# Two 16-head attentions in a four-layer kernel: order of the maxima, value projections for two pairs at a time, and the bank in which the maxima are turned

## The reference

```python
# first attention, causal
q = einsum('ahe,bce->bach', W_Q, x); k = ...W_K; v = ...W_V
scores = einsum('bach,baCh->bacC', k, q)
masked = where(causal, scores, -1e10)
attn = softmax(masked / sqrt(64)); z = einsum('bacC,baCh->bach', attn, v)
out = einsum('aeh,bach->bce', W_O, z)
x = layernorm(x + out)
# second attention of 16 heads, after the gated one
scores = einsum('bqhd,bkhd->bhqk', q, k) * (1/sqrt(16)) + rel_bias[buckets]
out = einsum('bhqk,bkhd->bqhd', softmax(scores), v).reshape(b, s, 1024) @ Wo
x = layernorm(x + out)
```

## Time and profile before

| | |
|---|---|
| median of 3 runs | 4945.93 us |
| the profiled execution | 4944.16 us, its span 4942.6 us |
| TensorE, matmuls | 4153.5 us busy (84%) |
| VectorE | 3627.2 us (73%) |
| GpSimd | 3000.0 us (61%) |
| ScalarE | 1976.0 us (40%) |
| mean granted TensorE clock | 0.926 |

### The profile page before, as it was taken

How to read it: one execution, slowest core, us unless ns; L and a number is a source line. 1 busy time by engine, 2 the same in 40 slices (tenths; PEclk the granted TensorE clock), 3 DMA queues, 4 the chain that set the end, 5 groups by cost and what they waited for, 6 DMA issues and landing times. The chain is left out here.

```text
span 4942.6 us, 63340 instructions
## 1 busy us (share of the span) xinstructions
PE 4153.5 (84%) x22330; PEld 2157.3 (44%) x22330; DVE 3627.2 (73%) x5957; ACT 1976.0 (40%) x3403; POOL 3000.0 (61%) x2548
## 2 busy tenths in 40 slices
PE   5999999999688788778778756999999999999947
PEld 3544544445354444444344323444444444444416
DVE  3877878777477677777777745888788788878735
ACT  2443434434264445345334322444344344434410
POOL 1655656556376787787778762666566566656710
PEclk6999999999889899899999976999999999999976
DMA  2000100000110000000000002212121121211120
GB/s 48 13 13 13 32 10 26 9 5 1 35 49 17 17 25 25 25 17 25 29 17 17 5 21 45 39 26 35 33 32 30 30 40 26 39 31 26 17 60 18
DMA packets 98044, 125.91 MB, mean 25 GB/s; under 512 B 28896, under 2 KB 76448, under 8 KB 97728
## 3 DMA queue, kind: packets, MB, share of 16 engines
q1 hardware_dynamic: 97728, 121.86, 11.5%
HBM read 103.69 MB, written 18.12 MB: 25 GB/s over the span
## 5 line engine op out<-in xcount | busy, mean ns | idle before, releaser
L777 POOL TENSOR_TENSOR s_psum_p<-s_psum_p,s_prob 128x1024 f32<-128x1024 f32 (+3 forms) x640 | 1350.3, 2110 | 418.2 <-ACT s_prob L524 379.7
L524 ACT ACTIVATE s_prob<-s_sT 128x1024 f32<-128x1024 f32 (+2 forms) x896 | 835.9, 933 | 972.4 <-DVE s_sT L658 477.3
L432 PE MATMUL s_pv<-s_prob,s_vp 128*64 128x512 f32 (+3 forms) x3584 | 888.7, 574 | 3.9 <-POOL s_prob L762 3.0
L777 POOL TENSOR_TENSOR s_psum_p<-s_prob 128x1024 f32<-128x1024 f32 (+1 forms) x128 | 286.8, 2241 | 576.7 <-ACT s_prob L524 574.0
L663 DVE RECIPROCAL s_recip<-s_recip 128x128 f32<-128x128 f32 x512 | 480.8, 941 | 99.2 <-ACT s_recip L474 99.2
L388 PE MATMUL s_mx<-s_bh,s_ah 64*128 64x512 f32 (+3 forms) x1792 | 390.8, 432 | 183.4 <-DVE s_bm L599 84.9
L1656 POOL TENSOR_TENSOR s_psum_p<-s_psum_p,s_prob 128x1024 f32<-128x1024 f32 x192 | 462.1, 2407 | 136.2 <-ACT s_prob L1377 134.5
L609 DVE CUSTOM_DVE_ANT_0 s_mx<-s_mx,s_strip 128x512 f32<-128x512 f32 x640 | 429.1, 711 | 112.0 <-PE s_mx L388 110.8
L407 PE MATMUL s_sT<-s_ah,s_bh 64*128 64x512 f32 (+3 forms) x1792 | 415.8, 460 | 19.0 <-ACT s_prob L524 18.7
L599 DVE TENSOR_REDUCE s_bm<-s_mx 128x8 f32<-128x1024 f32 (+3 forms) x384 | 362.3, 944 | 51.9 <-PE s_mx L388 43.1
L1377 ACT ACTIVATE s_prob<-s_sT 128x1024 f32<-128x1024 f32 x256 | 265.0, 1035 | 300.1 <-PE s_sT L1230 298.4
(11 more groups left out here) (242 smaller groups left out, 8475.6 us busy)
## 6 DMA issues: line engine op xcount, KB each, us to landing
s_strip<-bias_rows SPq DMA_DIRECT2D x256, 144.0 KB, 5.8
s_wr<-gated_weights SPq DMA_DIRECT2D x32, 960.0 KB, 4.9
s_near<-bias_rows SPq DMA_DIRECT2D x256, 48.0 KB, 2.0
x<-s_x SPq DMA_DIRECT2D x12, 512.0 KB, 3.2
s_x<-x SPq DMA_DIRECT2D x8, 512.0 KB, 5.0
gated_weights<-s_side_hi SPq DMA_DIRECT2D x8, 480.0 KB, 2.5
gated_weights<-s_side_lo SPq DMA_DIRECT2D x8, 480.0 KB, 2.9
s_x<-in_L_attn_x_dram SPq DMA_DIRECT2D x4, 512.0 KB, 4.5
```

Of the source, the lines that this page charges most:

```text
L432: last = mm(pv[heads(hd), lo:CH], vp[:, g % 2, j, heads(hd)], prob[:, k % PR, hd, lo:CH], start=j == 0, stop=end)
L524: nc.scalar.activation(prob[:, k % PR, :, lo:CH], sT[:, k % 2, :, lo:CH], ACT.Exp, scale=st.scale).then_inc(exp_done, 1)
L777: nc.gpsimd.tensor_tensor(out[:, :, lo:CH], src, p[:, :, lo:CH], ALU.add)\
```

## The change

Three things are changed in `jobs` and `pair_stage`.

The maxima: `mx_steps` is gone. Chunks n = 2 and on of pair g+1 stand one in each unit of pair g, from unit 0, and chunks 0 and 1 of pair g+2 stand in the last two units of pair g. The turning stays in its unit.

The values: a "v" job now makes the values of two pairs for two token blocks, with matmuls of 256 columns. Two pairs have four such jobs, and all four stand in the odd pairs. ScalarE takes each out with two copies, one for each pair, into a ring of three. In the pairs around a change of batch the other jobs move to the freed places.

The turning: the transpose goes to `misc` instead of `mx`. It waits for the reader of the job before it there, and the next job waits for `max_rows`; the chunks no longer do.

```diff
-        self.mx_steps = [1, 1, 2, 1, 2, 1, 1, 1, 1, 1, 0, 0] if causal else \
-            [1, 1, 1, 1, 1, 1, 2, 1, 2, 1, 2, 1, 1, 0, 0, 0]
...
-        value = lambda u, k: out[u].append(("v", g + 1, k)) if g + 1 < GP else None
+        value = lambda u, k: out[u].append(("v", (g + 1) // 2, k)) if g % 2 and g + 1 < GP else None
...
+            for n in range(self.NMX if g == 0 else self.NMX - 2):
+                u, k = (n, n + 2) if g > 0 else (n // 2, n) if n < 4 else (n - 2, n)
+                out[u].append(("mx", g + 1, k))
+            out[self.mt_unit].append(("mt", g + 1, 0))
+        if g + 2 < GP:
+            for n in range(2):
+                out[self.U - 2 + n].append(("mx", g + 2, n))
...
             if turn:
-                plan = {"v": (3, 4), "xt": (5, 7), "item": (8, 9, 10, 11)}
+                plan = {"v": (), "xt": (0, 1), "item": (3, 4, 7, 8)}
             elif after:
-                plan = {"item": (0, 1, 3, 4), "v": (5, 7), "y": (8, 9), "t": (10, 11)}
+                plan = {"item": (0, 1, 3, 4), "v": (), "y": (7, 8), "t": (9, 11)}
             else:
-                plan = {"item": (0, 1, 3, 4), "v": (8, 10)}
+                plan = {"item": (0, 1, 3, 4), "v": (5, 7, 8, 10)}
         else:
             if turn:
-                plan = {"v": (3, 5), "xt": (7, 8), "item": (9, 11, 13, 15)}
+                plan = {"v": (), "xt": (0, 1), "item": (3, 5, 7, 9)}
             elif after:
-                plan = {"item": (0, 1, 3, 4), "v": (5, 6), "y": (8, 9), "t": (11, 12)}
+                plan = {"item": (0, 1, 3, 4), "v": (), "y": (8, 9), "t": (11, 12)}
             else:
-                plan = {"item": (0, 3, 5, 7), "v": (8, 12)}
+                plan = {"item": (0, 3, 5, 7), "v": (1, 8, 11, 13)}
...
-        vp = sb("vp", [P, 2, NB, P])
+        vp = sb("vp", [P, 3, NB, P])
...
+                elif kind == "mt":
+                    pe.wait_ge(rows_done, 2 * of + 2)
...
-                    for n in range(4):
-                        o, rows = misc[:, n * P:(n + 1) * P], slice((4 * k + n) * P, (4 * k + n + 1) * P)
+                    p = 2 * of % NPAIR
+                    cols = slice(p * P, (p + 2) * P)
+                    for n in range(2):
+                        o, rows = misc[:, 2 * n * P:2 * (n + 1) * P], slice((2 * k + n) * P, (2 * k + n + 1) * P)
                         mm(o, xh[:, rows], wv[:, 0, cols], start=True, stop=False)
-                        mm(o, xl[:, rows], wv[:, 0, cols], start=False, stop=False)
-                        last = mm(o, xh[:, rows], wv[:, 1, cols], start=False, stop=True)
+                        mm(o, xh[:, rows], wv[:, 1, cols], start=False, stop=False)
+                        last = mm(o, xl[:, rows], wv[:, 0, cols], start=False, stop=True)
...
-                    pe.wait_ge(rows_done, 2 * g)
...
             def m_transpose(g):
+
+                nonlocal before
+                misc_free()
+                before = ("mt", g, 0)
                 pe.wait_ge(m_step, m_per * (g + 1))
-                nc.tensor.transpose(mx[:, 0, 0:P], m8[:, g % 2, :, :].rearrange("p a n -> p (a n)"),
+                nc.tensor.transpose(misc[:, 0:P], m8[:, g % 2, :, :].rearrange("p a n -> p (a n)"),
...
+                    both = misc[:, :].rearrange("p (i a n) -> p i a n", i=2, a=2)
+                    for a in range(2):
+                        copy(vp[:, (2 * of + a) % 3, 2 * k:2 * k + 2, :], both[:, :, a, :]).then_inc(v_done, 1)
```

More of the change, by code:

```diff
@@ L154, in jobs @@
         item = lambda u, k: out[u].append(("item", g + 2, k)) if g + 2 < GP else None
-        value = lambda u, k: out[u].append(("v", g + 1, k)) if g + 1 < GP else None
-        n = 0
+        value = lambda u, k: out[u].append(("v", (g + 1) // 2, k)) if g % 2 and g + 1 < GP else None
         if g + 1 < GP:
-            for u, count in enumerate(self.mx_steps):
-                out[u] += [("mx", g + 1, n + k) for k in range(count)]
-                n += count
-            out[self.mt_unit].append(("mt", g + 1))
+            for n in range(self.NMX if g == 0 else self.NMX - 2):
[5 more added lines that the diff above has]
+                out[self.U - 2 + n].append(("mx", g + 2, n))
         turn = p == NPAIR - 2 and b + 1 < B
@@ L431, in values @@
                 for hd in range(2):
-                    last = mm(pv[heads(hd), lo:CH], vp[:, g % 2, j, heads(hd)], prob[:, k % PR, hd, lo:CH],
+                    last = mm(pv[heads(hd), lo:CH], vp[:, g % 3, j, heads(hd)], prob[:, k % PR, hd, lo:CH],
                               start=j == 0, stop=end)
@@ L440, in _ @@
                 misc_job(("item", 0, k))
-            for k in range(2):
+            for k in range(4):
                 misc_job(("v", 0, k))
@@ L459, in _ @@
                     maxima(t[1], t[2])
[L460 removed]
+                if ("mt", g + 1, 0) in todo:
                     m_transpose(g + 1)
@@ L492, in misc_job @@
                 elif kind == "v":
-                    act.wait_ge(v_full, 2 * of + k + 1)
-                    if of >= 2:
-                        act.wait_ge(pv_done, (of - 1) * U)
-                    copy(vp[:, of % 2, 4 * k:4 * k + 4, :].rearrange("p i n -> p (i n)"), misc[:, :])\
-                        .then_inc(v_done, 1)
+                    act.wait_ge(v_full, 4 * of + k + 1)
+                    if of >= 1:
+                        act.wait_ge(pv_done, (2 * of - 1) * U)
+                    both = misc[:, :].rearrange("p (i a n) -> p i a n", i=2, a=2)
+                    for a in range(2):
+                        copy(vp[:, (2 * of + a) % 3, 2 * k:2 * k + 2, :], both[:, :, a, :]).then_inc(v_done, 1)
                 elif kind == "xt":
```

8 lines of the change are left out of this document (3 added, 5 removed).

## The result

| | before | after |
|---|---|---|
| median of four runs each | 4945.51 us | 5027.82 us (5023.22 to 5032.52) |
| ratio, 95% interval | | 1.0165 [1.0148, 1.0183] |
| span of the profiled execution | 4942.6 us | 5031.0 us |
| mean granted TensorE clock | 0.926 | 0.902 |

The account below looks back on a forecast made before the run. TensorE was taken as the busiest engine in both attentions, with VectorE's queue around the turning late next. Changes of -8 us (second attention) and -17 (first) took the profiled 4944.2 to 4919, median 4921; range 4850 to 4985.

Parts of the forecast that it names:

- one queue: VectorE's queue around the turning: in the second attention it shrinks a gain of 5.5 us a pair to 0.8.
- the clock behind the wait: Clock drops behind the new waits, partly absorbed by small waits: 1.1 us a pair in the second attention, 1.35 in the first.
- the waits of units 0 to 10: Second attention, even pair: 31.5 us plus 0.7 of waits; odd pairs add 1.7 of value jobs and a 0.45 wait.
- the pairs with other jobs: Second attention: transposes -1.4 us, output jobs -3.8, layer norm +1 a pair; first: transposes -3, output jobs -4.7.
- Value matmuls 0.12 us apart: Spacing of value matmuls of 256 columns, making a value job 0.85 us and saving 1.26 us a pair.
- TensorE's wait in unit 15: Second attention, every pair: TensorE stands 2.8 us until VectorE has read the pair-after-next's first chunk.
- units 11 to 15 of an even pair: Second attention: these units take 16.9 us by VectorE's queue, where TensorE's own work is 12.15.
- the turning behind the value job in the first attention: Odd pairs: the turning, wanting the same bank, waits 0.8 us for the two copies of the value job ahead.
- odd pairs of the first: First attention: an odd pair takes 35.55 us before the term for clock drops, which is 1.35 a pair.
- The copy of constants: VectorE's 2.21 us copy near the turning, 32 elements, held until GpSimd's add ends, in the second attention's queue.
- First attention: Usual pairs 35.65 us against 35.4 with the clock; with the other pairs, -17 us for the whole stretch.
- Rival 3: Second attention, unit 15: GpSimd's add starts first, holds the normalisation 2.3 us, 1.6 left a pair: 4971 us; chance 0.25.

Follow-up runs that it names:

- e9: The changed kernel with the copy of constants and the addition of delta moved from VectorE to ScalarE in unit 6: 4932.93 us, ratio 0.9981.
- e12: The kernel before with the copy of constants and the addition of delta moved from VectorE to ScalarE in unit 6: 4918.72 us, ratio 0.9959.
- e4: The changed kernel with 18 score matmuls repeated in unit 15 of the second attention, where TensorE waits: 4974.71 us, ratio 1.0058.
- e13: The changed kernel with GpSimd's additions in the second attention cut to 16 columns, most sums of exponentials left out: 4906.80 us, ratio 0.9930.
- e2: The kernel before with only the new chunk order and the turning's new bank, values for one pair at a time: 5121.03 us, ratio 1.0353.

## Why the prediction was wrong

**The direction.** I had a sum of small gains against one queue. The queue was as worked out; what failed are the terms laid beside it, nearly all missed on the same side: the clock behind the wait (1.1 us a pair, it was 1.9), the waits of units 0 to 10, and the pairs with other jobs. The miss is 107 us (4921 to 5028), some 78 in the second attention and 31 in the first.

**What held.** Value matmuls 0.12 us apart; TensorE's wait in unit 15, 2.69 for 2.8; units 11 to 15 of an even pair, 17.1 us for 16.9 (17.74 on the mean, less 0.65 for what unit 15 ran at 1.2 GHz); the turning behind the value job in the first attention, 0.75 for 0.8; odd pairs of the first, 36.86 for 36.9. The copy of constants was named as what makes the queue late, and e9 and e12 show that it and the addition behind it make 71 of the 82 us, with the clock drops that they brought.

**The clock** ("these absorb some: 1.1 us a pair in the second"). Nothing was absorbed: where the drop comes at once, as behind pair 3, it costs 1.2 us in unit 15 (6.52 with its wait of 2.69, against 4.20 with 1.57 in e9 at 2.4 GHz) and 1.05 in the next unit 0 (4.33 for 3.28), 2.2 in all; over the usual pairs the mean is 1.9. The wait that ends a pair is followed by TensorE's own work at 1.2 GHz, not by another wait. e4's 1.7 a pair fits this. The term should have been 1.9 and not 1.1, which makes 17 us over 21 usual pairs.

**Units 0 to 10** ("31.5 plus 0.7 of waits"). They took 33.1 us for 32.2 in even pairs, 34.5 for 33.7 in odd ones, the clock's share left out: 18 us over 21 pairs. In even pairs it is mostly unit 9: a wait of 0.39, which I had not counted, and 3.02 us from start to start, where a unit with a chunk and no wait takes 2.37. A wait of 0.4 thus costs 0.65. In odd pairs it is unit 8's value job, which waits 0.38 for VectorE (3.73 for 3.23), and unit 5 (3.60 for 3.28). My odd sum was also added up short: with the 0.7 of waits that the even pair has, 31.5, 0.7, 1.7, 0.45 and 17.4 make 51.75, and I wrote 51.1. With the clock, a usual pair of the second attention costs 2.4 us more than before on the mean, where I had 0.3: 44 us, of which these two terms are 35.

**The other pairs.** I had +1 for a layer-norm pair, and it was 7.3 by the table: 19 us. The step treated the layer norm as work of fixed length laid beside one more chunk. In fact the shifted order put three of its instructions beside GpSimd's additions, 2.2, 2.2 and 1.2 us longer each, and e13 takes all of it back (51.94). I had -3.8 and -1.4 for the pairs with output jobs and transposes; they gave -0.3 and +1.0, since unit 15's wait and drop come there too: 17 us.

**First attention.** It came out 31 us over the forecast (+14 for -17), 19 of them in usual pairs. In even pairs I had 34.4 with the clock, and they take 36.25. The waits are mostly as worked out: 1.87 us in unit 9 for 1.7, at most 0.36 in unit 10 for 0.5, and 1.4 to 1.6 in unit 11 in seven of nine pairs. But in pairs 4, 10, 12 and 26 the clock fell behind unit 9's wait as well, and in pairs 4 and 10 unit 11 then waited 3.69 and 3.42. What makes that wait grow is not worked out. In the output pairs, -0.6 for -4.7, 12 us more.

**Rival 3** (the normalisation of unit 15 held behind GpSimd's addition) named what happened: 2386 ns on the mean of 62, against 1364. Its price did not hold. Going from e9 to e13, which frees the normalisations and all the rest, gains 32 us of the second attention, 19 of them in layer-norm pairs; I had put 50 on usual pairs. After the change no wait of TensorE follows it in units 0 and 1, and in e9, with the clock at 2.4 GHz, 0.65 us do. The sum should have had both, the queue's hold and this one, not the one or the other.

The Trainium skill, "SBUF — State Buffer", section "🔬 SBUF: two separate sides", gives the shared port pair to one engine for a whole instruction, and names VectorE's modes that use both ports beside instructions with two SBUF inputs. By that rule the additions and multiplications are subject to it, and the copy and the scaling of 8 elements if they run in such a mode, so that the next of them can be caught when one is moved. The runs agree, with 2.22 us for the copy, 2.38 for the scaling and 2.20 for the addition of 6 elements. What my expectations called "two operands in SBUF" is too narrow for the copy and the scaling, which have one input.

Left open: how the first attention's loss divides between the bank and the order of the chunks, since e2 holds both; and the 1.57 us chain at unit 15, which no run with the chunks of after took away.

## What to carry to other kernels

When the orders of two engines shift against each other, price every small SBUF-to-SBUF copy, scaling, addition and multiplication of VectorE as if a GpSimd instruction could hold it to its end, and look which of them come before something that TensorE waits for. Removing one of them tests nothing if the next one is of the same kind; shorten the GpSimd instruction instead to see what all of them cost. And a wait of TensorE that stands in every pair costs its own length and the slow work behind it, so that filling it with repeated matmuls can be a gain and tells the two apart. Look then at what else the added work delayed: in e4 it also freed a held instruction.
